# Softmax probabilities divided by GpSimd alone, in one instruction for each group of heads

## The chip, the cores and the metric

The kernel runs on one core of one Trainium2 chip, in one launch. The metric is the time of the whole kernel on the device, in microseconds, as the median of the timed runs.

## The reference

Eight sequences of 128 tokens and 256 channels pass through cross attention and then a mixture of experts. Cut to what matters here:

```python
q = rms_norm((LN(x) @ wq)); k = rms_norm((LN(x) @ wk)); v = LN(x) @ wv       # 16 query heads, 4 key heads, width 128
k_ctx = rms_norm(ctx @ wk_ctx); v_ctx = ctx @ wv_ctx                         # 128 context tokens
q, k = rotary(q), rotary(k)
scores = q @ concat(k_ctx, k).T / sqrt(128) + causal_mask                    # 128 x 256 for each head
probs  = softmax(scores)                                                     # exp(s - max) / sum
x = x + (probs @ concat(v_ctx, v)) @ wo
x = x + moe(LN(x))                                                           # 8 experts, top 2, and a shared one
```

The place in question is the division in softmax: each of the 4 x 128 x 256 exponentials of a group of heads is multiplied by the reciprocal of its row's sum.

## The kernel before

One row of tokens lies in each of the 128 partitions. The outer loop runs over the eight sequences, `b` = 0 to 7; sequence 0 and sequence 7 are written out, and sequences 1 to 6 are a hardware loop on each engine. Inside it four groups `g` = 0 to 3 are written out, each with one key head and the R = 4 query heads that share it. `u` = 4b + g counts groups. After the attention the experts follow, on all sequences together.

Every engine has its own list of instructions, in an order fixed by hand, and the lists meet at semaphores only. The work of a group is staggered: while group g is in softmax, the queries of group g + 2 are projected and rotated, those of g + 1 are transposed, and the probabilities of g - 1 are transposed and multiplied with the values.

For one group the chain is this:

- TensorE computes the scores (`scores`, L1278) into `sc_ps`; VectorE takes their maximum (`scores_max`, L954, L957) and makes the bias `nbias` (L961).
- ScalarE makes the exponentials, one head at a time, into `probs` (L531), with the sums in `den`.
- VectorE waits for `s_exp`, makes the reciprocal `rden` (`normalise` on VectorE, L963 to L971) and then divides heads one by one (L970): two of four heads in groups 0, 1 and 3, all four in group 2.
- GpSimd waits for `s_rden` and divides the other two heads in one instruction over 512 elements a partition (`normalise` on GpSimd, L741, L744); in group 2 it divides none.
- TensorE transposes the probabilities in its next group (`turn_probs`, L1310, L1318), after waiting for both parts. It stands behind `q_turn` (L1247, L1263), the transposes of the next group's rotated queries. ScalarE and VectorE then split the transposed probabilities into a high and a low half (`p_copy`, L442; `p_low`, L895), and `mix` (L1328) multiplies them with the values.

GpSimd's list in a loop sequence (`row` on GpSimd, L782) is, by group:

- group 0: `q_add` (L758, the rotated queries of group 2), `normalise`, `q_roots` (L706, L708), the roots of the next sequence's layer norm (L699 to L714);
- group 1: `ln_low` (L719), `normalise`, `q_add`, `q_roots`, the root of the second norm;
- group 2: `kc_roots` (L706, L708), `q_add` (the queries of the next sequence's group 0), `k_roots`, `k_scale` (L737), `q_roots`;
- group 3: `q_add` (the next sequence's group 1), `normalise`, `q_roots`.

Sequence 0 differs: there `q_add` stands first in every group, and GpSimd also scales and splits half of the output weights (L809 in group 1, L814 in group 3). Sequences 1 to 3 carry casts of the expert weights (L831).

What else touches the steps: TensorE's `q_turn` of group 0 of the next sequence waits for GpSimd's `q_add` and for ScalarE's `kc_scale` (L501), which waits for GpSimd's `kc_roots`. TensorE's `k_turn` (L1227) waits for GpSimd's `k_scale`. TensorE's `q_turn` for group 2, which it issues in group 1, waits for VectorE's `v_low` (L927). In group 1 of every sequence but the first TensorE also does the output projection of the sequence before (`out_proj`, L1332, 48 matmuls).

Of the kernel before, what the change touches and what calls it, by code (L numbers as in the profile page):

```python
# [5 lines left out]
ALU = mybir.AluOpType  # L6
# [6 lines left out]
P = 128  # L13
# [17 lines left out]
def seen(eng, sem, count):  # L31

    if isinstance(count, int) and count <= 0:
        return
    eng.wait_ge(sem, count)
# [9 lines left out]
def xattn_moe_kernel(nc, x, ctx, wq, wk, wv, wo, wk_ctx, wv_ctx, q_norm_w, k_norm_w,  # L45
# [5 lines left out]
    R = H // G  # L51
# [8 lines left out]
    with ExitStack() as stack:  # L60
        def sb(name, shape, dt=F32):
            return stack.enter_context(nc.sbuf_tensor(name, shape, dt))

        def sem(name):
            return stack.enter_context(nc.semaphore(name))
# [92 lines left out]
        rden = sb("rden", [P, R])  # L158
        probs = sb("probs", [P, R, 2 * P])
# [135 lines left out]
        s_exp = sem("s_exp")  # L295
        s_rden = sem("s_rden")
        s_probs = sem("s_probs")
        s_probs2 = sem("s_probs2")

        def heads_dve(g):  # L300
            return R if g == 2 else R // 2

        def count_pool(b, g):
            return 3 * b + (0, 1, 2, 2, 3)[g + 1]
        p_turned = sem("p_turned")
        p_high = sem("p_high")
        p_ready = sem("p_ready")
# [367 lines left out]
        def _(pool):  # L675
# [64 lines left out]

            def normalise(b, g):  # L741
                pool.wait_ge(s_rden, G * b + g + 1)
                nv = heads_dve(g)
                nc.gpsimd.tensor_tensor(probs[:, nv:R, :], probs[:, nv:R, :],  # L744
                                        rden[:, nv:R].unsqueeze(2).broadcast_to([P, R - nv, 2 * P]),
                                        ALU.mult).then_inc(s_probs2, 1)

            def q_roots(b, g):
                u = G * b + g
# [32 lines left out]
            def row(b, first, last, cast=None):  # L782
                for g in range(G):
                    if g == 1 and not last:
                        ln_low(b + 1)
                    if (g in (0, 3) or first) and ahead_of(b, g, 2, last):
                        q_add(*ahead_of(b, g, 2, last))
                    if g == 0 and first:
                        ln_root(b + 1)
                    if g != 2:  # L790
                        normalise(b, g)
                    if g == 2 and not last:
                        kc_roots(b + 1)
                    if ahead_of(b, g, 2, last):
                        if g in (1, 2) and not first:
                            q_add(*ahead_of(b, g, 2, last))
                        if g != 2:
                            q_roots(*ahead_of(b, g, 2, last))
                    if g == 0 and not first and not last:
                        ln_root(b + 1)  # L800
                    if g == 1 and not first:
                        l2_root(b - 1)
                    if g == 2 and not last:
                        k_roots(b + 1)
                        k_scale(b + 1)
                        q_roots(b + 1, 0)
                    if first and g == 1:
                        pool.wait_ge(d_wo, 16)
                        nc.gpsimd.tensor_tensor(wo32[:, own_wo, :], wo32[:, own_wo, :],  # L809
                                                scale_w[:].unsqueeze(2).broadcast_to([P, H // 2, D]),  # L810
                                                ALU.mult).then_inc(wo_scaled, 1)
                    if first and g == 3:
                        pool.wait_ge(wo_high, 4)
                        nc.gpsimd.tensor_tensor(wo_lo[:, own_wo, :], wo32[:, own_wo, :], wo_hi[:, own_wo, :],  # L814
                                                ALU.subtract).then_inc(wo_low2, 1)
                    if cast:
                        for i in cast_slots[g]:
                            cast(i)
# [43 lines left out]
        def _(dve):  # L862
# [100 lines left out]
            def normalise(b, g):  # L963
                u = G * b + g
                dve.wait_ge(s_exp, u + 1)
                seen(dve, s_probs2, count_pool(b, g - 1))
                nc.vector.reciprocal(rden[:], den[:]).then_inc(s_rden, 1)  # L967
                dve.wait_ge(s_rden, u + 1)
                for h in range(heads_dve(g)):
                    last = nc.vector.tensor_scalar(probs[:, h, :], probs[:, h, :], rden[:, h:h + 1], None, ALU.mult)  # L970
                last.then_inc(s_probs, 1)  # L971

            def p_low(u):
                for a in range(2):
# [193 lines left out]
        def _(pe):  # L1168
# [141 lines left out]
            def turn_probs(b, g):  # L1310

                u = G * b + g - 1
                pe.wait_ge(s_probs, u + 1)
                pe.wait_ge(s_probs2, count_pool(b, g - 1))
                seen(pe, p_ready, 2 * u)
                for a in range(2):
                    for h in range(R):
                        last = nc.tensor.transpose(pt_ps[:, a, h * P:(h + 1) * P], probs[:, h, a * P:(a + 1) * P],  # L1318
                                                   ident[:])
                last.then_inc(p_turned, 1)  # L1320
# [282 lines left out]
```

## Time and profile before

| | |
|---|---|
| time before, median of 3 runs | 381.09 us (379.98 to 385.2) |
| span of the profiled execution | 381.2 us |
| TensorE busy | 343.1 us, 90% |
| VectorE busy | 331.7 us, 87% |
| ScalarE busy | 271.3 us, 71% |
| GpSimd busy | 191.6 us, 50% |

In the views PE is TensorE's matmuls, DVE is VectorE, ACT is ScalarE and POOL is GpSimd. L744 is line 744 of the kernel. Matmuls overlap each other, so a busy TensorE is not one at its peak. Ends of idle time are put down to whoever released the engine last.

### The profile page before, as it was taken

To read this page: it belongs to the slowest core of one execution; us is meant where nothing else is said; L and a number is where in the kernel's file an instruction comes from. 1 tells how busy PE (TensorE), PEld (TensorE's weight loads), DVE (VectorE), ACT (ScalarE), POOL (GpSimd) and SP (SyncE) were. 2 spreads that over 40 slices of the span, in tenths; PEclk is the share of its full clock that TensorE was granted. 3 is DMA by queue.
4 is the path that set the end of the run, shared out by engine and by line. 5 is a ranking of instruction groups with operands and counts; after the bars stand their busy time and mean duration, and the time that the engine had idled before them with its cause. 6 is when DMAs were issued, how large, how long until landed. Compare 5 with 4: busy or idle time off the path is not lost.

```text
span 381.2 us, 7816 instructions
## 1 busy us (share of the span) xinstructions
PE 343.1 (90%) x2471; PEld 235.3 (62%) x2476; DVE 331.7 (87%) x577; ACT 271.3 (71%) x913; POOL 191.6 (50%) x266
## 2 busy tenths in 40 slices
PE   6678697699999989999999999999999999988994
PEld 5354455376567666866685577558666768664572
DVE  1687999998999899899989998999899896759653
ACT  3667879576986797698759876986797566067562
POOL 3377666663766386528454554655284401234330
PEclk9998989999999999999999999999999998999998
DMA  5966000000030003000000000000000000000011
GB/s 174 379 208 220 17 0 0 3 2 14 3 110 0 14 0 110 15 0 0 0 14 0 0 0 14 0 0 0 0 0 1 2 0 2 2 0 3 13 45 56
DMA packets 11604, 13.50 MB, mean 35 GB/s; under 512 B 824, under 2 KB 9024, under 8 KB 11584
## 3 DMA queue, kind: packets, MB, share of 16 engines
q1 hardware_dynamic: 11584, 13.25, 10.7%
q8 instruction: 10, 0.16, 0.2%
q14 instruction: 10, 0.08, 0.1%
HBM read 12.20 MB, written 1.05 MB: 35 GB/s over the span
## 4 chain that ended last, share of the span: by engine, by line
DVE 40%; PE 34%; issue 12%; ACT 6%; POOL 3%; DMA 2%; SPq 1%; DVEq 1%; ACTq 0%; POOLq 0%
PE proj L1342 10%; DVE probs L970 9%; DVE nmax L957 6%; DVE pT_lo L895 4%; PE pt_ps L1318 3%; DVE q_t L886 3%; PE proj L1174 3%; PE o_ps L1328 3%; PE sc_ps L1284 3%; DVE q_t L888 3%; DVE qT_lo L895 2%; ACT probs L531 2%; PE turn L1263 2%; DMA wq<-in_L_xattn_wq_dram 2%; PE proj L1506 2%
## 5 line engine op out<-in xcount | busy, mean ns | idle before, releaser
L531 ACT ACTIVATE probs<-sc_ps,nbias,q_r 128x256 f32<-128x256 f32 x128 | 70.8, 574 | 3.4 <-DVE nbias L961 3.4
L758 POOL TENSOR_TENSOR q_rot<-q_t 128x512 f32<-128x512 f32 x32 | 42.8, 1336 | 36.2 <-DVE q_t L888 35.4
L970 DVE TENSOR_SCALAR probs<-probs,rden 128x256 f32<-128x256 f32 x80 | 57.1, 763 | 1.1
L442 ACT ACTIVATE pT_hi<-pt_ps 128x512 f16<-128x512 f32 x64 | 34.8, 597 | 14.5 <-PE pt_ps L1318 14.5
L1174 PE MATMUL proj<-wq_hi,xT 128*128 128x512 f16 x128 | 39.2, 389 | 3.4 <-DVE wq_lo L879 3.0
L895 DVE SCALAR_TENSOR_TENSOR pT_lo<-pt_ps,pT_hi 128x512 f16<-128x512 f32 x64 | 40.9, 680 | 1.2 <-ACT pT_hi L442 1.2
L475 ACT ACTIVATE q_junk<-proj 128x128 bf16<-128x128 f32 x128 | 34.0, 296 | 9.5 <-DVE q_t L888 9.5
L957 DVE TENSOR_REDUCE nmax<-sc_ps 128x4 f32<-128x1024 f32 x32 | 38.8, 1212 | 1.5 <-PE sc_ps L1306 1.5
L1318 PE MATMUL pt_ps<-ident,probs 128*128 128x128 f32 x256 | 34.9, 281 | 2.2 <-DVE probs L970 2.0
L708 POOL TENSOR_TENSOR q_r<-q_me,power 128x4 f32<-128x4 f32 x32 | 34.2, 1069 | 2.5
L1342 PE MATMUL proj<-wo_hi,oT_hi 128*128 128x256 f16 x128 | 34.9, 273 | 0.0
L1342 PE MATMUL proj<-wo_lo,oT_hi 128*128 128x256 f16 x128 | 34.9, 273 | 0.0
L1342 PE MATMUL proj<-wo_hi,oT_lo 128*128 128x256 f16 x128 | 34.9, 273 | 0.0
L442 ACT ACTIVATE qT_hi<-turn 128x512 f16<-128x512 f32 x32 | 19.5, 610 | 21.3 <-PE turn L1263 21.3
L744 POOL TENSOR_TENSOR probs<-probs,rden 128x512 f32<-128x512 f32 x24 | 25.3, 1055 | 17.0 <-DVE rden L967 16.5
L847 POOL TENSOR_TENSOR wq<-xn_all,weight 128x512 bf16<-128x512 f32 x16 | 17.1, 1071 | 33.1 <-DVE weight L1115 13.0
L1318 PEld LDWEIGHTS pt_ps<-ident,probs 128*128 128x128 f32 x256 | 29.5, 144 | 4.1 <-issue 3.0
L1263 PE MATMUL turn<-ident,q_rot 128*128 128x128 f32 x128 | 19.9, 278 | 12.5 <-POOL q_rot L758 6.2
L475 ACT ACTIVATION_READ_ACCUMULATOR q_junk<-proj 128x1 f32 x128 | 28.7, 228 | 0.0
L531 ACT ACTIVATION_READ_ACCUMULATOR probs<-sc_ps,nbias,q_r 128x1 f32 x128 | 27.7, 216 | 0.0
L1328 PE MATMUL o_ps<-pT_hi,v_hi 128*128 128x512 f16 x64 | 24.3, 379 | 3.1 <-DVE pT_lo L895 3.1
L895 DVE SCALAR_TENSOR_TENSOR oT_lo<-o_ps,oT_hi 128x512 f16<-128x512 f32 x32 | 21.8, 680 | 5.3 <-ACT oT_hi L442 5.3
(217 smaller groups left out, 940.6 us busy)
## 6 DMA issues: line engine op xcount, KB each, us to landing
wq<-in_L_xattn_wq_dram SPq DMA_DIRECT2D x4, 512.0 KB, 8.8
w<-in_L_ffn_w_dram SPq DMA_DIRECT2D x2, 1024.0 KB, 10.2
wq<-in_L_xattn_wo_dram SPq DMA_DIRECT2D x1, 2048.0 KB, 8.4
ctx_b<-in_ctx_dram SPq DMA_DIRECT2D x8, 128.0 KB, 2.0
out_dram<-x_all SPq DMA_DIRECT2D x4, 256.0 KB, 2.2
x_all<-in_x_dram SPq DMA_DIRECT2D x1, 896.0 KB, 12.6
wkc<-in_L_xattn_wk_ctx_dram SPq DMA_DIRECT2D x1, 512.0 KB, 4.1
wk<-in_L_xattn_wk_dram SPq DMA_DIRECT2D x1, 512.0 KB, 5.0
```

Of the source, the lines that this page charges most:

```text
L442: return nc.scalar.activation(out_, in_, ACT.Copy, scale=scale)
L475: last = nc.scalar.activation(junk[:, head], bank[:, head], ACT.Square, scale=scale, accum_out=dst[:, h:h + 1])
L531: last = nc.scalar.activation(probs[:, h, :], sc_ps[:, h, :], ACT.Exp, bias=nbias[:, h:h + 1], scale=q_r[:, g, h:h + 1], accum_out=den[:, ...
L708: nc.gpsimd.tensor_tensor(r, me, power[:], ALU.pow).then_inc(root, 1)
L758: nc.gpsimd.tensor_tensor(q_rot[:], q_t1[:], q_t2[:], ALU.add).then_inc(q_added, 1)
L895: return nc.vector.scalar_tensor_tensor(out=lo, in0=src, scalar=scale, in1=hi, op0=ALU.mult, op1=ALU.subtract)
L957: nc.vector.tensor_reduce(nmax[:], sc_ps[:], AX_X, ALU.max, negate=True).then_inc(s_max, 1)
L970: last = nc.vector.tensor_scalar(probs[:, h, :], probs[:, h, :], rden[:, h:h + 1], None, ALU.mult)
L1174: last = nc.tensor.matmul(bank[:], xT[:, a, c, :], w[:, c, cols], start=(n == 0), stop=(n == 3 * DC - 1))
L1318: last = nc.tensor.transpose(pt_ps[:, a, h * P:(h + 1) * P], probs[:, h, a * P:(a + 1) * P], ident[:])
L1328: last = nc.tensor.matmul(o_ps[:], v[:, a, g * P:(g + 1) * P], p[:, a, :], start=(a == 0 and i == 0), stop=(a == 1 and i == 2))
L1342: last = nc.tensor.matmul(proj[0][:, 0:D], o[:, h // R, (h % R) * P:(h % R + 1) * P], w[:, h, :], start=(h == 0 and i == 0), stop=(h == H ...
```

## The change

GpSimd's `normalise` divides all four heads with one instruction over 1024 elements a partition, and it does so in all four groups, group 2 too, where it takes its place ahead of `kc_roots`. VectorE's `normalise` keeps the reciprocal and loses the divisions: two in groups 0, 1 and 3, four in group 2. One semaphore, `s_probs`, now raised by GpSimd, takes the place of two. VectorE waits on it before it overwrites `rden`, and TensorE before it transposes.

```diff
--- before.py
+++ after.py
@@ -295,13 +295,6 @@
         s_exp = sem("s_exp")
         s_rden = sem("s_rden")
         s_probs = sem("s_probs")
-        s_probs2 = sem("s_probs2")
-
-        def heads_dve(g):
-            return R if g == 2 else R // 2
-
-        def count_pool(b, g):
-            return 3 * b + (0, 1, 2, 2, 3)[g + 1]
         p_turned = sem("p_turned")
         p_high = sem("p_high")
         p_ready = sem("p_ready")
@@ -740,10 +733,8 @@
 
             def normalise(b, g):
                 pool.wait_ge(s_rden, G * b + g + 1)
-                nv = heads_dve(g)
-                nc.gpsimd.tensor_tensor(probs[:, nv:R, :], probs[:, nv:R, :],
-                                        rden[:, nv:R].unsqueeze(2).broadcast_to([P, R - nv, 2 * P]),
-                                        ALU.mult).then_inc(s_probs2, 1)
+                nc.gpsimd.tensor_tensor(probs[:], probs[:], rden[:].unsqueeze(2).broadcast_to([P, R, 2 * P]),
+                                        ALU.mult).then_inc(s_probs, 1)
 
             def q_roots(b, g):
                 u = G * b + g
@@ -787,8 +778,7 @@
                         q_add(*ahead_of(b, g, 2, last))
                     if g == 0 and first:
                         ln_root(b + 1)
-                    if g != 2:
-                        normalise(b, g)
+                    normalise(b, g)
                     if g == 2 and not last:
                         kc_roots(b + 1)
                     if ahead_of(b, g, 2, last):
@@ -963,12 +953,8 @@
             def normalise(b, g):
                 u = G * b + g
                 dve.wait_ge(s_exp, u + 1)
-                seen(dve, s_probs2, count_pool(b, g - 1))
+                seen(dve, s_probs, u)
                 nc.vector.reciprocal(rden[:], den[:]).then_inc(s_rden, 1)
-                dve.wait_ge(s_rden, u + 1)
-                for h in range(heads_dve(g)):
-                    last = nc.vector.tensor_scalar(probs[:, h, :], probs[:, h, :], rden[:, h:h + 1], None, ALU.mult)
-                last.then_inc(s_probs, 1)
 
             def p_low(u):
                 for a in range(2):
@@ -1311,7 +1297,6 @@
 
                 u = G * b + g - 1
                 pe.wait_ge(s_probs, u + 1)
-                pe.wait_ge(s_probs2, count_pool(b, g - 1))
                 seen(pe, p_ready, 2 * u)
                 for a in range(2):
                     for h in range(R):
```

## Rows read from the trace of the kernel before

**Rows 1.** TensorE, VectorE and the rest: the page's busy time, share and instructions

```profile
PE 343.1 (90%) x2471; PEld 235.3 (62%) x2476; DVE 331.7 (87%) x577; ACT 271.3 (71%) x913; POOL 191.6 (50%) x266
```

**Rows 2.** Busy time in one sequence, then in its group 1 (stretch, length, engines)

```profile
161.96:197.96 36.00, 34.48 (x248) 23.77 (x247) 34.58 (x62) 28.34 (x107) 20.04 (x28) 1.00 0.01 4
...
223.50:233.88 10.38, 10.38 (x89) 8.26 (x88) 9.29 (x18) 6.47 (x23) 5.29 (x9) 1.00 0.04 13
```

**Rows 3.** TensorE's waits from 90 to 300 us (who for whom: total, times, longest)

```profile
PE turn L1263 <- POOL q_rot L758: 3.2, 6, 0.5
PE turn L1263 <- DVE v_lo L895: 2.0, 6, 0.4
PE proj L1231 <- POOL k_rot L737: 1.9, 6, 0.3
PE pt_ps L1318 <- DVE probs L970: 1.1, 5, 0.3
```

**Rows 4.** Timeline of GpSimd, groups 2, 3 and 0 (start, length, engine, line)

```profile
203.71 0.36 POOL L706 TENSOR_TENSOR kc_me<-kc_ss,eps_kc 128x4 f32<-128x4 f32 x1 [6.68 <-ACT kc_junk L475]
204.15 1.02 POOL L708 TENSOR_TENSOR kc_r<-kc_me,power 128x4 f32<-128x4 f32 x1
205.14 1.27 POOL L758 TENSOR_TENSOR q_rot<-q_t 128x512 f32<-128x512 f32 x1
...
212.70 1.04 POOL L744 TENSOR_TENSOR probs<-probs,rden 128x512 f32<-128x512 f32 x1
...
219.25 1.26 POOL L758 TENSOR_TENSOR q_rot<-q_t 128x512 f32<-128x512 f32 x1 [4.22 <-DVE q_t L888]
```

**Rows 5.** Timeline of VectorE, groups 2, 3 and 0

```profile
202.66 0.18 DVE L967 RECIPROCAL rden<-den 128x4 f32<-128x4 f32 x1
202.87 1.14 DVE L970 TENSOR_SCALAR probs<-probs,rden 128x256 f32<-128x256 f32 x4
...
212.45 0.17 DVE L967 RECIPROCAL rden<-den 128x4 f32<-128x4 f32 x1
212.66 1.50 DVE L970 TENSOR_SCALAR probs<-probs,rden 128x256 f32<-128x256 f32 x2
...
221.73 0.65 DVE L895 SCALAR_TENSOR_TENSOR v_lo<-turn,v_hi 128x512 f16<-128x512 f32 x1
```

**Rows 6.** All divisions on VectorE: shortest, median and longest, ns

```profile
L970 DVE TENSOR_SCALAR probs<-probs,rden x80: 340/584/1376, 34.2 to 316.9; 128x256 f32<-128x256 f32 x80
```

**Rows 7.** Groups of instructions by shape (busy us, mean ns, idle before)

```profile
L970 DVE TENSOR_SCALAR probs<-probs,rden 128x256 f32<-128x256 f32 x80 | 57.1, 763 | 1.1
...
L744 POOL TENSOR_TENSOR probs<-probs,rden 128x512 f32<-128x512 f32 x24 | 25.3, 1055 | 17.0 <-DVE rden L967 16.5
...
L814 POOL TENSOR_TENSOR wo_lo<-wq,wo_hi 128x2048 f16<-128x2048 f32 x1 | 4.2, 4215 | 0.0
L809 POOL TENSOR_TENSOR wq<-wq,scale_w 128x2048 f32<-128x2048 f32 x1 | 3.6, 3596 | 0.0
```

**Rows 8.** Timeline of TensorE and ScalarE, groups 2, 3 and 0

```profile
206.49 0.63 PE L1263 MATMUL turn<-ident,q_rot 128*128 128x128 f32 x4 [0.54 <-POOL q_rot L758]
...
214.38 1.09 PE L1318 MATMUL pt_ps<-ident,probs 128*128 128x128 f32 x8 [0.20 <-DVE probs L970]
...
220.69 0.60 ACT L442 ACTIVATE v_hi<-turn 128x512 f16<-128x512 f32 x1 [0.42 <-PE turn L1174]
...
222.53 0.63 PE L1263 MATMUL turn<-ident,q_rot 128*128 128x128 f32 x4 [0.34 <-DVE v_lo L895]
```

**Rows 9.** Timeline of VectorE and TensorE: sequence 0 first, then sequence 7

```profile
48.99 2.37 DVE L961 TENSOR_TENSOR nbias<-nmax,q_r 128x4 f32<-128x4 f32 x1
...
311.13 1.09 PE L1318 MATMUL pt_ps<-ident,probs 128*128 128x128 f32 x8
...
315.56 0.18 DVE L967 RECIPROCAL rden<-den 128x4 f32<-128x4 f32 x1 [0.77 <-ACT probs L531]
...
317.33 1.67 PE L1318 MATMUL pt_ps<-ident,probs 128*128 128x128 f32 x8 [0.44 <-DVE probs L970]
```

## What the change will do to the time

> **What bounds the kernel now.** I read the page's busy times first. TensorE is busy for 90% of the span and VectorE for 87%, GpSimd for 50% [rows 1]. That looks like a case for moving work from VectorE to GpSimd, so the next question is which of the two busy engines sets the end. One sequence of the loop takes 36.0 us, and in it TensorE is busy for 34.48 us and VectorE for 34.58 us [rows 2]. In group 1, where TensorE has the 48 matmuls of the output projection, it is busy for 10.38 of 10.38 us. No work taken from VectorE can shorten that group.
>
> The list of TensorE's waits shows what is left to gain. From 90 to 300 us it waits 3.2 us for GpSimd's `q_rot`, 2.0 us for VectorE's `v_lo`, 1.9 us for GpSimd's `k_rot` and 1.1 us for VectorE's divisions [rows 3]. That is 8.2 us over some six sequences, 1.4 us in each. Of these, 5.1 us are waits for GpSimd and 3.1 us for VectorE. So the kernel hangs on TensorE, and where TensorE waits, it waits more for GpSimd, the engine that receives work, than for the one that loses it.
>
> **What VectorE loses.** The 80 divisions take 57.1 us, 763 ns each [rows 7]. That mean is no price of the work: the shortest takes 340 ns and the longest 1376 ns [rows 6]. In group 2, where GpSimd divides nothing, four run in 1.14 us; in group 3, beside GpSimd's division, two take 1.50 us [rows 5]. Most of a long one is waiting for GpSimd. The rule of the Trainium skill (SBUF — State Buffer, "Who interferes with whom") is that the two engines share a pair of ports under an exclusive lock, taken by a VectorE instruction in a 2-port mode or with two SBUF inputs; the trace agrees, 340 ns alone against 1376 ns. Per sequence the chain loses about 1.1 us of VectorE in group 2 and 1.4 to 2.4 us in each other group. What that is worth depends on who waits for VectorE afterwards, below.
>
> **What GpSimd gains.** The trace has no division over 1024 elements. GpSimd's multiply by a broadcast operand takes 1.04 us for 512 elements [rows 4] and 3.60 us for 2048 [rows 7]. The line through both has (3.60 - 1.04)/1536 = 1.67 ns an element, so 1024 elements take 1.04 + 512 x 0.00167 = 1.89 us. Bounds: without any fixed part it would be 1024 x 0.00167 = 1.71 us; at the rate of the subtraction with two full operands, 4.215 us for 2048 [rows 7], it would be 2.11 us. I take 1.89 us, since both rows behind it are of the same kind.
>
> A rule of the Trainium skill speaks against the change: GPSIMD Engine Reference, section 3.1, gives 4497 ns for a `tensor_tensor` over 2048 elements and keeps elementwise work on VectorE. By that figure an instruction of 1024 would take about 2.2 us, an estimate, and the sum below would come to about 12 instead of 7 us. The rows have 3.60 us for 2048 elements where one operand is a broadcast, so the sum does not go by it.
>
> **The steps on the chain, one loop sequence.** Times are those of the profiled execution.
>
> *Group 2.* VectorE's reciprocal ends at 202.66 + 0.18 = 202.84 [rows 5]. GpSimd follows a reciprocal by 0.08 us (212.45 + 0.17 to 212.70) [rows 4, 5], so its new division runs from 202.92 to 204.81. Until now it sat idle for 6.68 us here and began `kc_me` at 203.71 [rows 4], when ScalarE's squares came. Now `kc_me` and `kc_r` start behind the division. From start to start they take 0.28 us (the 0.36 holds a wait for VectorE's last division, gone now) and 0.99 us, so `q_rot` starts at 204.77 + 0.28 + 0.99 = 206.04 instead of 205.14: 0.90 us later. The squares do not get the cover back, because TensorE begins to transpose `q_rot` 0.08 us after it ends and had been idle 0.54 us for it [rows 8]. TensorE is thus 0.9 us late at its `q_turn`. Behind it stand the transposes of the probabilities, ScalarE's copies and the exponentials of group 3; `kc_n` and the squares of k are late by as much, so `k_roots` and `k_rot` are too. The 1.14 us taken from VectorE here buy nothing: its next product on this path waits for ScalarE. VectorE's `k_sum`, which now starts beside GpSimd, may hold `q_rot` another 0.15 us.
>
> *Group 3.* The exponentials and with them the reciprocal move from 212.62 to 213.52. The division runs 213.60 to 215.49, and TensorE can transpose at 215.56. Before it began at 214.38 [rows 8]. So the delay grows to 1.18 us: the single instruction of 1.89 us is longer than the two divisions beside each other, 1.50 us.
>
> *Group 0.* The projection of v ends 1.18 us later. ScalarE's `v_hi`, which waits for it [rows 8], runs from 221.87 to 222.47. VectorE took `v_lo` at 221.73 [rows 5], held until then by its divisions, 0.44 us after `v_hi` ended. Now it can follow at once, to about 223.1, and TensorE's `q_turn`, 0.15 us behind it, starts at about 223.3 instead of 222.53 [rows 8]. This is the one place where VectorE's relief pays: the delay shrinks to about 0.75 us. The division of group 0 follows `q_rot`: 219.25 + 1.26 + 1.18 = 221.69 [rows 4], to 223.55, and is needed 0.46 us after `q_turn` starts, at 223.75. It is hidden by 0.2 us, and every 0.1 us on the division beyond that is paid.
>
> *Group 1.* The division is hidden behind the output projection: TensorE wants its result some 4 us after it ends. If that cover were gone it would cost its 1.89 us. TensorE is full here [rows 2], so nothing of the 0.75 us is won back either.
>
> With part of the 0.15 us I take 0.85 us a sequence, six times: 5.1 us.
>
> **Sequence 0.** VectorE bounds it, and here it gains: its two divisions of group 1 stand ahead of `cT_lo`, for which TensorE waits. On the other side small products on VectorE stand still while GpSimd holds the ports: `nbias` took 2.37 us in group 1 of sequence 0 [rows 9], as it came during the multiply of 3.60 us. The same happens in front of sequence 1 with the subtraction of 4.2 us [rows 7], which now starts up to 1.3 us later, since division and roots come first. I set the gain of group 1 to 0.5 us against that 1.3 us: +0.8 us, with -0.5 and +3 as bounds.
>
> **Sequence 7.** In group 2 the four divisions are bare: reciprocal at about 309.9, division to 311.86, TensorE at 311.93 instead of 311.13 [rows 9]: 0.8 us. In group 3 the reciprocal ends at 315.74, the division at 317.71, TensorE goes on at 317.78 instead of 317.33 [rows 9]: 0.45 us. What follows waits for TensorE and moves along. Sum 1.25 us.
>
> **The sum**, against the span of 381.2 us, which is 0.1 us from the median: 5.1 + 0.8 + 1.25 = 7.2 us, so 388.4 us, 1.9% slower.
>
> **Rivals.**
>
> *The division is slower, or the ports collide.* With 2.11 us instead of 1.89 the steps of groups 2 and 3 grow by 0.22 us each, group 0 loses its 0.2 us of cover, and a sequence costs 1.2 us: 7.2 us in six, 1.7 us in sequence 7, and up to 3 us in sequence 0: 393 us. For it: VectorE's work with two SBUF operands can make GpSimd wait as well. Against it: GpSimd's own divisions scatter little, 1055 ns on average [rows 7].
>
> *It is hidden.* If `q_rot` were not what TensorE needs first in group 2, only 0.3 us of group 3 would be left, VectorE's relief would cancel it, and the time would be 382 us. For it: VectorE's list is nearly full, and a good part of the 381.2 us could follow from its order. Against it: the wait for `q_rot` is the largest of TensorE's [rows 3].
>
> *VectorE was the bound, and the kernel gets faster.* The mechanism is the wait for `v_lo` together with that for the divisions in groups 3 and 0, 3.1 us in six sequences [rows 3], and in sequence 0 some 3 us of VectorE's chain: 375 us at best, and under 373.5 us (2%) only if the waits for GpSimd shrank too. It decides if GpSimd's division in group 2 ends before ScalarE's squares do, at 203.7; it would have to take 0.8 us. Nothing in the rows allows that.
>
> **How the numbers follow.** Chances: the forecast 0.55, with a range of its own from 385 to 391.5; slower division or collisions 0.2; hidden 0.18; faster 0.07. The range from 382 to 393.5 leaves out the faster case and the tail of the slow one. A change of 2% is about what a measurement of this kernel can tell from none, and 2% slower is 388.7 us, close to my forecast. A little under half of the forecast's chance lies above it, with the slow rival 0.45 in all. Faster by over 2% gets 0.03 of the 0.07. The rest, 0.52, is within 2%.
>
> **What the profile would show.** GpSimd's division at 1.85 to 1.95 us, 32 times; in group 2 no idle time before `kc_me`, and TensorE's idle time before `q_turn` there up from 0.54 to about 1.4 us; TensorE waiting for GpSimd's probabilities in group 3 for about 0.5 us; no wait for `v_lo` in group 0; group 1 unchanged at 10.4 us; a sequence of 36.7 to 36.8 us against 36.0 [rows 2]. VectorE's busy time falls by 55 us and its idle time grows by more. The forecast is wrong if `q_rot` in group 2 is not late by 0.9 us, if group 0 uncovers the division, or if sequence 0 moves by over 2 us.

## The result and the profile after

| | before | after |
|---|---|---|
| median of the timed runs | 380.89 us (379.98 to 385.20) | 390.52 us (390.19 to 391.38) |
| ratio, with its 95% interval | | 1.0244 [1.0188, 1.0300] |
| span of the profiled execution | 381.2 us | 388.5 us |
| one loop sequence, from output projection to output projection | 35.90 us | 36.96 us |

The changed kernel is 2.4% slower; by the interval it can be 1.9 or 3.0%. The times rose by 9.6 us and the two profiled spans differ by 7.3 us. These are two different questions, answered in two places below.

First the page: the busy times and, under them, the shares of the chain that ended last.

```profile
PE 342.8 (88%) x2471; PEld 235.1 (61%) x2476; DVE 277.9 (72%) x497; ACT 271.2 (70%) x913; POOL 226.6 (58%) x274
...
PE 47%; DVE 17%; POOL 15%; issue 9%; ACT 7%; DMA 2%; SPq 1%; DVEq 0%; POOLq 0%; ACTq 0%
```

VectorE lost 53.8 us of work against [rows 1] and GpSimd gained 35.0, and the kernel got longer. TensorE does the same work (342.8 us against 343.1), so the 7.3 us are idle time of TensorE. Its list of waits, here from 90 to 310 us, says for whom:

```profile
PE turn L1249 <- POOL q_rot L749: 9.8, 6, 1.6
PE pt_ps L1303 <- POOL probs L736: 3.2, 6, 0.6
PE sc_ps L1270 <- ACT probs L524: 1.6, 6, 0.3
```

Set against [rows 3], over six sequences: the wait for `q_rot` grew from 3.2 to 9.8 us; the probabilities, now GpSimd's, cost 3.2 instead of 1.1; a wait for ScalarE's exponentials of 1.6 us is new, and those for `v_lo` (2.0) and `k_rot` (1.9) are gone. The sum of the differences is 6.6 + 2.1 + 1.6 - 2.0 - 1.9 = 6.4 us. The six sequences together grew by 6.34 us: 221.75 us from the first to the last of their output projections, against 215.41. The list accounts for all of it, to 0.1 us.

Where in a sequence it happens, the timelines say. Sequence 3 starts here 2.88 us later than before, so 2.88 is to be taken from these times before they are set beside [rows 4, 5, 8]. GpSimd in groups 2 and 3:

```profile
205.75 1.89 POOL L736 TENSOR_TENSOR probs<-probs,rden 128x1024 f32<-128x1024 f32 x1 [5.25 <-DVE rden L957]
207.60 0.20 POOL L699 TENSOR_TENSOR kc_me<-kc_ss,eps_kc 128x4 f32<-128x4 f32 x1
207.88 1.02 POOL L701 TENSOR_TENSOR kc_r<-kc_me,power 128x4 f32<-128x4 f32 x1
208.87 1.55 POOL L749 TENSOR_TENSOR q_rot<-q_t 128x512 f32<-128x512 f32 x1
...
216.66 1.89 POOL L736 TENSOR_TENSOR probs<-probs,rden 128x1024 f32<-128x1024 f32 x1 [0.16 <-DVE rden L957]
```

TensorE in groups 2, 3 and 0 of the same stretch:

```profile
210.47 0.66 PE L1249 MATMUL turn<-ident,q_rot 128*128 128x128 f32 x4 [1.64 <-POOL q_rot L749]
...
218.69 1.09 PE L1303 MATMUL pt_ps<-ident,probs 128*128 128x128 f32 x8 [0.55 <-POOL probs L736]
...
226.46 0.63 PE L1249 MATMUL turn<-ident,q_rot 128*128 128x128 f32 x4
```

The division stands directly ahead of `kc_me`, with no idle time between. TensorE reaches `q_turn` in group 2 at 207.59 by before's clock of events (210.47 - 2.88), 1.10 us later than before, after waiting 1.64 us instead of 0.54. In group 3 it is 1.43 us late (215.81 against 214.38), in group 0 1.05 us (223.58 against 222.53), with no wait for `v_lo` left. Group 1 takes 10.38 us, to the hundredth what it took before [rows 2], and hands the 1.05 us on.

**The remaining parts of the 7.3 us.** The first output projection starts at 81.37 us, before at 81.58: sequence 0 gives 0.21 us back. From the last output projection of the loop to the end it is 85.4 us against 84.2: 1.2 us. So -0.21 + 6.34 + 1.2 = +7.3 us.

### The profile page after: what moved, and what is told of

It reads as the page before. It is cut to its first block, busy times and chain, and to the rows that moved or that the text cites. A ratio compares the mean times of both kernels' runs of the same rounds, so it can differ in the third digit from the quotient of the medians.

```text
span 388.5 us, 7713 instructions
## 1 busy us (share of the span) xinstructions
PE 342.8 (88%) x2471; PEld 235.1 (61%) x2476; DVE 277.9 (72%) x497; ACT 271.2 (70%) x913; POOL 226.6 (58%) x274
## 3 DMA queue, kind: packets, MB, share of 16 engines
HBM read 12.20 MB, written 1.05 MB: 34 GB/s over the span
## 4 chain that ended last, share of the span: by engine, by line
PE 47%; DVE 17%; POOL 15%; issue 9%; ACT 7%; DMA 2%; SPq 1%; DVEq 0%; POOLq 0%; ACTq 0%
PE proj L1327 9%; POOL probs L736 6%; PE pt_ps L1303 6%; PE o_ps L1313 5%; POOL q_rot L749 5%; PE sc_ps L1270 5%; PE proj L1160 5%; PE turn L1160 3%; PE turn L1249 3%; DVE nmax L947 3%; PE proj L1173 2%; DVE q_t L876 2%; DVE q_t L878 2%; DMA wq<-in_L_xattn_wq_dram 2%; ACT probs L524 2%
## 5 line engine op out<-in xcount | busy, mean ns | idle before, releaser
L736 POOL TENSOR_TENSOR probs<-probs,rden 128x1024 f32<-128x1024 f32 x32 | 61.4, 1920 | 45.3 <-DVE rden L957 45.2
L749 POOL TENSOR_TENSOR q_rot<-q_t 128x512 f32<-128x512 f32 x32 | 45.1, 1408 | 28.8 <-DVE q_t L878 28.8
L701 POOL TENSOR_TENSOR q_r<-q_me,power 128x4 f32<-128x4 f32 x32 | 33.3, 1042 | 2.5
L885 DVE SCALAR_TENSOR_TENSOR qT_lo<-turn,qT_hi 128x512 f16<-128x512 f32 x32 | 21.9, 686 | 10.6 <-ACT qT_hi L435 10.5
L468 ACT ACTIVATION_READ_ACCUMULATOR q_junk<-proj 128x1 f32 x128 | 29.5, 239 | 0.0
L524 ACT ACTIVATION_READ_ACCUMULATOR probs<-sc_ps,nbias,q_r 128x1 f32 x128 | 28.5, 222 | 0.0
```

The costliest lines, as they stand in the source:

```text
L468: last = nc.scalar.activation(junk[:, head], bank[:, head], ACT.Square, scale=scale, accum_out=dst[:, h:h + 1])
L524: last = nc.scalar.activation(probs[:, h, :], sc_ps[:, h, :], ACT.Exp, bias=nbias[:, h:h + 1], scale=q_r[:, g, h:h + 1], accum_out=den[:, ...
L701: nc.gpsimd.tensor_tensor(r, me, power[:], ALU.pow).then_inc(root, 1)
L736: nc.gpsimd.tensor_tensor(probs[:], probs[:], rden[:].unsqueeze(2).broadcast_to([P, R, 2 * P]), ALU.mult).then_inc(s_probs, 1)
L749: nc.gpsimd.tensor_tensor(q_rot[:], q_t1[:], q_t2[:], ALU.add).then_inc(q_added, 1)
L885: return nc.vector.scalar_tensor_tensor(out=lo, in0=src, scalar=scale, in1=hi, op0=ALU.mult, op1=ALU.subtract)
```

## The experiments

The theory: TensorE is late because its next `q_rot` stands behind the new division in GpSimd's list (group 2), and because one division of 1.89 us is a longer way than two beside each other (group 3). The rivals: the effect is spread over all groups, through the ports; or VectorE's load is what matters; and, for the start, whether sequence 0 is neutral or hides two large effects.

For most runs the kernel before was rewritten so that a table says how many heads VectorE divides in each group, and GpSimd divides the others in one instruction. Before is (2, 2, 4, 2), the change is (0, 0, 0, 0). The kernels before and after were run again too. Ratios are to the kernel before in the same series of runs (its medians there lie between 380.89 and 382.27 us).

| heads on VectorE in groups 0, 1, 2, 3 | first output projection | a loop sequence | span | ratio [95%] |
|---|---|---|---|---|
| 2, 2, 4, 2 (before, again) | 82.06 | 35.90 | 380.0 | 1.0017 [0.9990, 1.0044] |
| 0, 0, 0, 0 (after, again) | 80.94 | 36.96 | 388.1 | 1.0241 [1.0188, 1.0294] |
| 2, 2, 0, 2 | 81.37 | 36.98 | 388.2 | 1.0266 [1.0220, 1.0313] |
| 2, 2, 2, 2 | 82.66 | 35.97 | 383.0 | 1.0043 [1.0020, 1.0065] |
| 0, 0, 4, 0 | 75.46 | 35.90 | 373.9 | 0.9875 [0.9834, 0.9916] |
| 0, 0, 4, 4 | 80.45 | 35.38 | 375.5 | 0.9887 [0.9844, 0.9929] |
| 4, 4, 4, 4 | 77.41 | 35.50 | 373.2 | 0.9865 [0.9821, 0.9909] |
| 0, 0, 4, 4 and `nbias` let through | 76.24 | 35.38 | 371.4 | 0.9794 [0.9738, 0.9850] |

The columns are not equally clean. In every profiled execution TensorE's granted clock is 1.00 from the first output projection to the last one of the loop, so a loop sequence compares like with like. Ahead of it and behind it the clock falls to its lower level, 1.2 GHz, in some stretches, and not at the same places each time. The pages show it for the kernel with group 2 undone, for the kernel before once more and for the one with two heads everywhere (tenths of the full clock in 40 slices):

```profile
PEclk9999999999999999999999999999999999999998
PEclk9998989989999999999999999999999999999999
PEclk9998989899999999999999999999999998999998
```

Up to the first output projection there is no such stretch in the first of these, one in after again, two in the first profiles of before and after, and three in the other two. The same kernel profiled twice differs by it and by its start-up: 81.58 and 82.06 us for before, 81.37 and 80.94 us for after. Differences of a few tenths in the second column, and of up to 2 us in the fourth, need therefore be no effect of an edit.

### After once more

No edit. Expected:

> The changed kernel again, on the chip of the next three, so that all are compared with the same runs. Theory (the delay of q_rot in group 2 and the division in group 3, on TensorE's path): span about 388.5 us and 36.97 us from one output projection to the next, as in its first profile. If the loss were noise of one execution, the distance would scatter from sequence to sequence and lie between 35.9 and 37.0.

The slowdown of the first result repeats, and 36.96 us a sequence with it.

### Group 2 undone, and group 2 alone

```diff
-        on_dve = (0, 0, 0, 0)
+        on_dve = (0, 0, 4, 0)      # first run
+        on_dve = (2, 2, 0, 2)      # second run
```

> One part of the change undone: in group 2 VectorE divides all four heads again and GpSimd none; GpSimd still divides all four in groups 0, 1 and 3. Theory: most of the loss comes from group 2. q_rot of group 2 is back at its old distance, the reciprocal of group 3 too; GpSimd's division there ends 0.28 us later than TensorE could start before, and VectorE's relief in group 0 gives about 0.4 us back. So 35.7 to 35.9 us a sequence instead of 36.97, and a span of 379.5 to 381.5 us. Rival (the slower instruction costs wherever it stands, or the shared ports do): three of four divisions are still GpSimd's, so three quarters of the 7.3 us stay: 386 to 387 us.

> One part of the change alone: GpSimd divides all four heads in group 2; groups 0, 1 and 3 stay split two and two. Theory: q_rot is 0.9 to 1.1 us late in every sequence and nothing gives it back, so 36.8 to 37.0 us a sequence, 1.3 to 1.6 us over that in sequences 0 and 7, and a span of 387 to 389 us. Rival (the loss is spread over the groups): a quarter of it, 383 us.

With VectorE dividing in group 2 alone, a sequence takes 35.90 us, exactly that of before. With GpSimd dividing in group 2 and all else as before, it takes 36.98 us, that of after. TensorE's list of waits for the second kernel has after's figure for `q_rot`, and the wait for `v_lo` is still there, since VectorE kept its other divisions:

```profile
PE turn L1269 <- POOL q_rot L763: 9.8, 6, 1.6
PE turn L1269 <- DVE v_lo L900: 2.6, 6, 0.5
PE sc_ps L1290 <- ACT probs L536: 1.6, 6, 0.3
```

So the whole loss of the loop is the division in group 2; taking the other three groups from VectorE neither cost nor gained anything there. That is a balance, not an absence of effects. With VectorE dividing in group 2 only, TensorE waits:

```profile
PE turn L1269 <- POOL q_rot L763: 3.3, 6, 0.5
PE pt_ps L1326 <- POOL probs L749: 2.7, 5, 0.6
PE proj L1237 <- POOL k_rot L742: 1.9, 6, 0.3
```

Against [rows 3], 1.6 us more for the probabilities of group 3 and 2.0 less for `v_lo`: what the long division loses in group 3, group 0 gives back.

The first kernel had a surprise. Its span is 373.9 us and not 379.5 to 381.5, and 6.1 of the 7.3 us that it is shorter than before stand ahead of the first output projection, at 75.46 us against 81.58. The other 1.2 us lie in the tail, where the granted clock was 1.00 here and 0.62 in the first profile of before. The experiment with `nbias`, below, is about the larger part.

### VectorE's divisions left out

The kernel before, with VectorE's divisions gone: its heads stay undivided in the output, and TensorE waits for the reciprocal in their place.

```diff
-                    for h in range(heads_dve(g)):
-                        last = nc.vector.tensor_scalar(probs[:, h, :], probs[:, h, :], rden[:, h:h + 1], None, ALU.mult)
-                    last.then_inc(s_probs, 1)
...
-                pe.wait_ge(s_probs, u + 1)
+                pe.wait_ge(s_rden, u + 1)
```

> What VectorE's divisions cost the kernel before: they are left out and nobody does them (the heads that VectorE divided stay undivided, so the output is not the reference's); GpSimd still divides its two heads in groups 0, 1 and 3, and TensorE waits for the reciprocal and for GpSimd. Theory (TensorE and the wait for q_rot set the pace, VectorE hardly): TensorE gains 0.35 us in group 3 and about 0.2 us in group 0, so 35.3 to 35.5 us a sequence, 1 to 3 us in sequence 0, 1.1 us in sequence 7: 374 to 377 us. Rival (VectorE at 87% is the bound): of its 57 us most comes back, so under 360 us.

The time fell to 372.70 us, 0.9761 [0.9722, 0.9799], and a sequence to 35.00 us. This bounds the gain from relieving VectorE: 0.9 us a sequence and some 9 us in all, if nobody else has to do the work. I had expected less from it, 0.4 to 0.6 us in the loop and 374 to 377 us in all. The 53.8 us that VectorE lost by the change could never have come back as time.

### The addition of k moved away

`k_sum` on VectorE starts 0.26 us before `q_rot` on GpSimd, and both read two operands from SBUF. The edit puts it behind the maximum in group 3.

```diff
                     scores_max(b, g)
+                    if g == 3 and not last:
+                        k_add(b + 1)
...
-                    if g == 2 and not last:
-                        k_add(b + 1)
```

> The changed kernel with VectorE's k_sum moved behind the maximum and nbias of group 3, where q_rot is over. Theory: in the changed kernel q_rot takes 1.55 us in group 2 instead of 1.27 because k_sum, with two operands in SBUF, holds the shared ports when q_rot comes; so q_rot is back at 1.27 us, TensorE waits 1.36 instead of 1.64 us for it, and a sequence takes 36.7 instead of 36.97 us: 1.7 us less in six sequences, a span of 386 to 387 us. Rival (q_rot is slowed by something else, or k_sum is now too late for k_rot): 36.97 us or more a sequence.

```profile
208.45 1.26 POOL L749 TENSOR_TENSOR q_rot<-q_t 128x512 f32<-128x512 f32 x1
...
PE turn L1249 <- POOL q_rot L749: 8.4, 6, 1.4
```

The first line is GpSimd's timeline, the second TensorE's list of waits. `q_rot` takes 1.26 us instead of 1.55, TensorE waits 1.4 us less for it over six sequences, and a sequence takes 36.76 us instead of 36.96. In the list `k_rot` is back with 1.9 us, and the 1.6 us for the exponentials are gone. The ratio is 1.0164 [1.0134, 1.0194]; the span fell to 385.8 us, more than the six sequences explain, because the granted clock in the tail was 1.00 here. So 0.20 of the 1.06 us is this meeting of the two additions. In the kernel before the two met the other way round. `q_rot` had started at 205.14, took 1.27 us [rows 4], and `k_sum` paid, as its line in VectorE's timeline shows:

```profile
205.73 1.23 DVE L946 TENSOR_TENSOR k_sum<-k_t 128x512 f32<-128x512 f32 x1
```

After, the division has pushed `q_rot` behind the start of `k_sum`, which takes 0.68 us, and `q_rot` pays.

### GpSimd's division behind the roots and the addition

After, with the division of group 2 moved from ahead of `kc_me` to behind `q_rot`.

```diff
-                    normalise(b, g)
+                    if g != 2:
+                        normalise(b, g)
                     if g == 2 and not last:
                         kc_roots(b + 1)
...
+                    if g == 2:
+                        normalise(b, g)
```

> The changed kernel with GpSimd's division of group 2 moved behind kc_roots and q_add, so that it still divides everything but holds nothing up. Theory (the place in the list is one price, the latency of the division another): q_rot is on time again, but the probabilities of group 2 are ready 1.3 to 1.4 us after TensorE wants them, so a sequence takes 37.2 to 37.5 us against 36.97 and the span is 389 to 392 us. Rival (only the delay of q_rot costs): 35.9 us a sequence and 376 to 382 us.

```profile
PE pt_ps L1307 <- POOL probs L736: 13.5, 12, 1.7
PE sc_ps L1274 <- ACT probs L524: 2.9, 6, 0.5
PE turn L1253 <- POOL q_rot L749: 2.3, 6, 0.4
```

The wait for `q_rot` is gone, and a larger one for the probabilities has taken its place: 37.61 us a sequence (37.2 to 37.5 were expected), 1.0262 [1.0198, 1.0326]. The whole is not later by six times that, because the first output projection starts at 78.73 us: `nbias`, the subject of the next experiment, was not held in sequence 0. So it is not a matter of order in GpSimd's list. In group 2 TensorE needs `q_rot` and the probabilities within a microsecond of each other, and GpSimd can't make both in time in either order.

### `nbias` let through before GpSimd's long subtraction

In group 3 of after's sequence 0, VectorE's `nbias` for group 0 of sequence 1, 4 elements a partition, runs beside GpSimd's `wo_lo`, 2048 elements a partition. VectorE's line first, then GpSimd's:

```profile
67.63 4.04 DVE L951 TENSOR_TENSOR nbias<-nmax,q_r 128x4 f32<-128x4 f32 x1
...
67.59 4.06 POOL L804 TENSOR_TENSOR wo_lo<-wq,wo_hi 128x2048 f16<-128x2048 f32 x1
```

GpSimd was 0.04 us earlier, and VectorE stood until it had ended. The Trainium skill (SBUF — State Buffer, "Who interferes with whom") has the port pair that the two engines share as an exclusive lock, for which a VectorE instruction with two SBUF inputs contends with a GpSimd instruction that reads SBUF. The trace agrees: 4.04 us against 0.16 us in the next run. One wait makes the order the other one:

```diff
                     if first and g == 3:
                         pool.wait_ge(wo_high, 4)
+                        pool.wait_ge(s_bias, G + 1)
                         nc.gpsimd.tensor_tensor(wo_lo[:, own_wo, :], wo32[:, own_wo, :], wo_hi[:, own_wo, :],
```

> The changed kernel with one wait more: in group 3 of sequence 0 GpSimd begins its subtraction over 2048 elements only when VectorE has made nbias of sequence 1's group 0. Theory: in the changed kernel nbias takes 4.04 us there, 3.9 us of them behind that subtraction, so the first output projection starts at about 77.5 us instead of 81.0 to 81.4, the loop stays at 36.97 us a sequence, and the span falls from 388.3 to about 384.5 us. That would also explain why one part undone gained 6 us before the loop. Rival (nbias is late for another reason, or something else is as late there): nothing moves.

```profile
67.59 0.16 DVE L952 TENSOR_TENSOR nbias<-nmax,q_r 128x4 f32<-128x4 f32 x1
...
67.90 4.08 POOL L805 TENSOR_TENSOR wo_lo<-wq,wo_hi 128x2048 f16<-128x2048 f32 x1 [0.32 <-DVE nbias L952]
```

The first output projection starts at 77.57 us instead of 81.37, the loop is unchanged at 36.96, and the ratio falls to 1.0120 [1.0094, 1.0146]. The span fell by 5.5 us; the rest beyond these 3.8 us is the tail, with its clock at 1.00.

The 3.8 us are not the hold alone. Behind it TensorE waited 2.74 us for `pT_lo`, in the kernel after and in its repetition alike, but what followed ran at different clocks. First the matmul behind the wait and the stretch around it in the kernel after, then the same two of after once more, where `nbias` was held for 4.05 us:

```profile
72.93 0.61 PE L1313 MATMUL o_ps<-pT_hi,v_hi 128*128 128x512 f16 x1 [2.74 <-DVE pT_lo L885]
71.00:76.50 5.50, 3.57 (x11) 1.36 (x12) 4.25 (x9) 3.44 (x16) 2.41 (x3) 0.69 0.00 0
```

```profile
73.49 0.39 PE L1313 MATMUL o_ps<-pT_hi,v_hi 128*128 128x512 f16 x1 [2.74 <-DVE pT_lo L885]
71.50:77.00 5.50, 3.51 (x21) 1.98 (x22) 4.39 (x10) 4.04 (x18) 2.41 (x3) 1.00 0.00 0
```

From the start of `nbias` to the first output projection it is 13.74 us in after, 12.75 in after once more and 9.98 with `nbias` let through. So the hold costs 2.8 us, and 1.0 us is the lower clock (granted 0.69 against 1.00). Whether the wait brings the lower clock is open: of the ten profiled executions in which TensorE waits 2.4 to 3.5 us at this place, six show it at the end of the wait or within 2 us behind it, and four don't.

The kernel before pays here too:

```profile
70.27 2.18 DVE L961 TENSOR_TENSOR nbias<-nmax,q_r 128x4 f32<-128x4 f32 x1
```

From there to its first output projection it is 11.31 us, at full clock. The change thus made this stretch 1.44 us longer, and the clock another 0.99. Ahead of it the changed kernel gained 2.64 us (67.63 against 70.27). Of these, 0.55 us were there before the first division (the first `nmax` starts at 27.93 us, in before at 28.48), and the lower clock has a part in the other 2.09, with two stretches in before and one in after. Together -0.55 - 2.09 + 1.44 + 0.99 = -0.21 us.

The surprise of the run with group 2 undone comes out of the same reckoning. There `nbias` started at 65.34 us and took 0.16 us, because GpSimd's subtraction came at 65.77, and 10.12 us followed up to the first output projection. So of the 5.9 us against after, 3.6 lie behind the start of `nbias` and 2.3 ahead of it, where the division of group 2 in sequence 0 is back on VectorE: TensorE reaches its `q_turn` there at 54.43 us, and at 56.74 in after. A part of these 2.3 us can be the clock, which fell once ahead of it in after and not at all here.

### Two heads on each engine in every group

```diff
-        on_dve = (2, 2, 4, 2)
+        on_dve = (2, 2, 2, 2)
```

> The dose between: in all four groups VectorE divides two heads and GpSimd two, so in group 2 GpSimd gets an instruction over 512 elements ahead of kc_roots. Theory: it runs from 0.08 us after the reciprocal for 1.04 us and ends 0.2 us after the squares for kc_me are ready, so q_rot is 0.2 to 0.4 us late and a sequence takes 36.1 to 36.3 us, against 35.90 with no head of group 2 on GpSimd and 36.97 with four. The price is no line through the two: the first 0.8 us are hidden by the idle time before kc_me. Rival (each head of group 2 on GpSimd costs the same): 36.4 us a sequence or more.

A sequence takes 35.97 us, 0.07 more than before, and less than I had expected (36.1 to 36.3). With 0, 2 and 4 heads of group 2 on GpSimd, a sequence takes 35.90, 35.97 and 36.98 us. GpSimd's idle time before `kc_me` swallows the short division almost whole, and not the long one. `q_rot` starts 0.05 us later than before here (206.47 us, in a sequence that begins 1.28 us later), and 0.85 us later in after. Up to that cover the division is nearly free; beyond it, it is paid.

### Whole groups on one engine

In group 3 VectorE's four divisions take 1.14 us if GpSimd divides nothing, and GpSimd's one takes 1.89. So groups 0 and 1, whose divisions are covered, go to GpSimd, and groups 2 and 3 to VectorE; the second run adds the wait of the `nbias` experiment, and the third gives all to VectorE.

```diff
+        on_dve = (0, 0, 4, 4)      # first and second run
+        on_dve = (4, 4, 4, 4)      # third run
```

> A version meant to beat both: GpSimd divides all four heads in groups 0 and 1, VectorE all four in groups 2 and 3. Theory: in group 3 VectorE alone needs 1.15 us where both together took 1.50 and GpSimd alone 1.89, so TensorE's wait of 0.55 us for the division there goes; group 0 keeps the early v_lo, group 2 its q_rot. 35.2 to 35.4 us a sequence against 35.90 before and 35.91 with group 2 undone. In sequence 0 GpSimd's subtraction may start earlier and hold nbias, so 369 to 374 us. Rival (VectorE, with eight divisions a sequence again, is late elsewhere): 35.9 us a sequence, 374 us or more.

> Groups 0 and 1 on GpSimd, groups 2 and 3 on VectorE, and GpSimd's subtraction over 2048 elements in sequence 0 held until VectorE has made nbias of sequence 1's group 0. Theory: without that wait nbias took 3.16 us there and the first output projection started at 80.45 us; with it that falls by 2.5 to 3 us, the loop keeps 35.39 us a sequence, and the span is 372 to 373 us. Rival (sequence 0 is bound by something else by now): 375 us.

> The mirror of the change: VectorE divides all four heads in every group and GpSimd none. Theory: without GpSimd's division beside it VectorE needs about 0.3 us a head, so 1.15 us in group 3 instead of 1.50, and TensorE's wait there goes; in group 0 q_rot holds the ports until 0.7 us after the reciprocal, so v_lo is about as late as before. 35.5 to 35.7 us a sequence, and a span of 376 to 380 us, faster than before although VectorE has more divisions to do. Rival (VectorE, the second busiest engine, pays for each division, 763 ns on average): 48 more divisions cost 36 us of VectorE, 390 us or more.

The first run, VectorE's timeline in group 3 and TensorE's waits:

```profile
209.96 1.14 DVE L976 TENSOR_SCALAR probs<-probs,rden 128x256 f32<-128x256 f32 x4
...
PE turn L1269 <- POOL q_rot L763: 3.2, 6, 0.5
PE proj L1237 <- POOL k_rot L742: 1.9, 6, 0.3
```

No probabilities and no `v_lo` are left in the list, and a sequence takes 35.38 us, as expected. The span was above what I expected, since `nbias` was held for 3.16 us in sequence 0 (and the clock fell three times ahead of the first output projection). With the wait the hold is gone: median 373.34 us against 381.45, ratio 0.9794 [0.9738, 0.9850]. The first output projection came 4.2 us earlier, more than the 2.5 to 3 us expected; 2.9 of them lie behind the start of `nbias`, and the other 1.3 ahead of it, where the clock fell once instead of twice. Of all kernels run that compute the whole result this is the fastest by its median, ahead of both before and after; whether it beats before by 2% the interval leaves open.

With all divisions on VectorE a sequence takes 35.50 us and the whole 376.26 us, 0.9865 [0.9821, 0.9909]. The page's busy times, and the divisions by shape:

```profile
PE 339.2 (91%) x2471; PEld 234.6 (63%) x2476; DVE 326.7 (88%) x625; ACT 271.0 (73%) x913; POOL 167.1 (45%) x242
...
L975 DVE TENSOR_SCALAR probs<-probs,rden 128x256 f32<-128x256 f32 x128 | 51.0, 460 | 1.1
```

VectorE divides 128 times here, in 51.0 us; before it divided 80 times, in 57.1 us [rows 7]. It has 48 more instructions and is busy 5 us less (326.7 against 331.7 [rows 1]). Before, GpSimd's help made the work that VectorE kept dearer by more than the work it took off. The Trainium skill (GPSIMD Engine Reference, "Engine selection") gives elementwise work to VectorE; this run agrees against both before and after. The mixed kernel with 35.38 us a sequence goes lower still in the loop, since groups 0 and 1 cost nothing on GpSimd: with them there TensorE's wait for `v_lo` (2.3 us over six sequences with all on VectorE) is gone.

### Before once more

No edit. Expected:

> The kernel before, profiled again. The forecast took the span of its first profile, 381.2 us, for its time; later executions on record span 378.3 to 381.2 us, 379.7 in the middle, and each takes 1.7 us more than it spans. Theory: the first profile was a slow one by about 1.5 us, and the loop is not where it scatters: again 35.9 us a sequence, and the difference lies before the first output projection (81.58 us then, 80 to 80.5 now) or behind the last (84.21 us then). Rival (the loop itself scatters): the distances between output projections move, which would put the comparison of loops in doubt.

The loop is the same to 0.02 us, and `nbias` was held for 2.37 and 2.18 us again. The first output projection was not earlier, as expected, but 0.48 us later, with three stretches of lower clock ahead of it instead of two. What makes the span shorter is the tail. The stretch behind the last transposed probabilities, in the kernel before, in it again, and in the kernel after (length, busy time of TensorE, its loads, VectorE, ScalarE, GpSimd, then the granted clock):

```profile
317.30:321.80 4.50, 4.47 (x33) 4.38 (x34) 2.82 (x5) 2.60 (x4) 0.00 (x0) 0.62 0.00 0
```

```profile
317.30:321.80 4.50, 4.06 (x39) 3.27 (x39) 3.88 (x8) 2.81 (x6) 0.06 (x1) 1.00 0.00 0
```

```profile
324.60:329.20 4.60, 4.51 (x33) 4.39 (x34) 1.69 (x3) 2.56 (x4) 0.03 (x1) 0.63 0.00 0
```

In the profiled execution on which the prediction rests, TensorE's granted clock was 0.62 there, which is most of the stretch at 1.2 instead of 2.4 GHz. In the one repeated it was 1.00, and the same work, from the last transposes to the router, was 1.66 us shorter. In both TensorE had waited 0.44 us directly ahead of it, so the profile doesn't show why the clock fell in one and not in the other. This stays open. The price of the change in the tail doesn't depend on it: from the last output projection of the loop to that of the last sequence it is 27.04 us in before and 28.28 in after, both with the lower clock, and 25.39 in before once more and 26.62 with `nbias` let through, both at 1.00.

## Why the prediction came out as it did

It said 388.4 us, from 382.0 to 393.5, and within 2% a little more likely than slower by more. The time was 390.52 us. The mechanism was the right one: the experiment with group 2 alone shows it with nothing else changed.

| step of the prediction | said | measured |
|---|---|---|
| division over 1024 elements | 1.89 us | 1.89 us, mean 1.92 |
| `q_turn` late in group 2 | 0.90 us, up to 0.15 more | 1.10 us |
| transposes late in group 3 | 1.18 us | 1.43 us |
| `q_turn` late in group 0 | 0.75 us | 1.05 us |
| group 1 | unchanged | 10.38 us, unchanged |
| a loop sequence | 36.7 to 36.8 us | 36.96 us |
| six sequences | +5.1 us | +6.34 us |
| up to the first output projection | +0.8 us | -0.21 us |
| tail | +1.25 us | +1.2 us |
| span | 388.4 us | 388.5 us |
| time above the span | 0 | 1.7 us |

That the span came out within 0.1 us is chance: two steps were off by about 1 us in opposite directions.

**The loop, 0.85 against 1.06 us.** The term that was too small is that of `k_sum`. The prediction named it, allowed up to 0.15 us and took a part of that. It was 0.28 us on `q_rot` (1.55 against 1.27), and the run that moves it away gives back 0.20 us a sequence. Before, `q_rot` was the first of the two and lost nothing; the prediction saw that the order would turn, but put too low a price on it and counted only a part of that. The rest of the group 3 step, 1.43 - 1.10 = 0.33 us against the 0.28 worked out, was right. The prediction took from 1.18 to 0.75 in group 0, a gain of 0.43, and 0.38 was measured.

**Sequence 0, +0.8 against -0.21 us.** Of its two terms the gain was the one that was too small: 0.5 us was set down, and up to `nbias` of the next sequence the changed kernel was 2.64 us ahead, 2.1 of them not in the start-up. The loss of up to 1.3 us measured 1.44, but this was in part luck. The prediction reckoned it as a subtraction that starts later; what happened is that `nbias`, held for 2.18 us in before, met the subtraction 0.04 us after its start and was held for all of it, 4.04 us. Had it got through, it would have been 2.8 us the other way. The lower clock behind the wait, 1.0 us in this execution, stood in no term.

**Span and time.** The sum was made against a span of 381.2 us, held to be within 0.1 us of the median. But the time of an execution lies above its span: after's profiled execution took 390.25 us with a span of 388.5, before's repeated one 381.71 with 380.0, both 1.7 us. By that a span of 381.2 belongs to a time of about 382.9 us, so the profiled execution of before was one of its long ones, with the clock of 0.62 in the tail. That time was not recorded; it is worked out from the 1.7 us. A forecast of 388.4 us for the span was one of 390.1 us for the time of such an execution, and this is why 390.52 us lies 2.1 us above the forecast. It does not make the forecast of the rise right: added to the median of before, 7.2 us would have given 388.1 us, and the medians rose by 9.6 us, with 7.2 to 11.4 us by the interval. The sum lies at the lower end of it. The traces account for the 7.3 us between two spans, not for the other 2.3. If before's other executions had the clock of 1.00 in the tail, as its second profile had, 1.66 of them would be that, since both profiles of after had the lower one; no trace shows what the other executions had. Since 2% slower begins at 388.7 us, the base also moved the balance between "within 2%" and "slower"; the interval leaves it open on which side of 2% the change lies.

**The rivals.** *Slower division or ports*: the division was not slower at all; the ports gave 0.2 us a sequence in the loop, and in sequence 0 a hold worth 2.8 us, of which before's own hold had been the smaller version. It held a part of the truth. *Hidden*: false, and the doses 0, 2 and 4 heads say why it was plausible. Two heads would have been hidden but for 0.07 us a sequence. *VectorE was the bound*: false for this change, but not empty. Relief of VectorE is worth 0.9 us a sequence when it is free. Here it was paid for at the one place where TensorE stood waiting for GpSimd.

## What to carry to other kernels

Before work is moved to an engine with idle time, look at what stands next in that engine's list and who waits for it: the idle time directly ahead of that instruction is the cover, here 0.9 us from the end of the reciprocal to `kc_me`, and of what the long division took beyond it, 1.1 us, nearly all was paid. In this kernel the two engines that share ports should not have split one small piece of work; it was better to give all of a group to one of them, to VectorE where TensorE waits, to GpSimd where the result is needed late. And compare times with times, spans with spans, and stretches outside the loop only with the granted clock beside them.

## What the hardware showed that I had not expected

- A VectorE multiplication of 4 elements a partition, 0.16 us alone, stood for 4.04 us behind a GpSimd instruction that had started 0.04 us earlier. Its release was worth 2.8 us at full clock, and 3.8 us with the lower clock that followed the wait in one execution.
- Which of two instructions is held can't be read from their starts alone. In before a division on VectorE started at 192.42 us and took 1.23 us instead of 0.34, although GpSimd's, 1.04 us long as ever, started at 192.46.
- Shared work was dearer than unshared: 128 divisions on VectorE in 51.0 us, 80 of them beside GpSimd's in 57.1.
- GpSimd's single division kept its price beside a busy VectorE, 1.92 us on average over 32, and 2.78 us at most, in sequence 0.
- The same kernel, the same stretch of its tail: granted clock 0.62 in one execution, 1.00 in another, 1.66 us apart.
